# A four-layer gated attention kernel: one weight load in four transfers, a result stored in eight pieces, and a new instruction order on four engines

## The chip, the cores and the metric

The kernel runs on one core of a Trainium2 chip, in one launch. The metric is the device time of that launch in microseconds (us); where several runs are given, their median counts.

## What is computed

The input x holds 8 batches of 128 tokens with 128 features (float32). Four layers follow one another. Each adds a gated cross-attention and then a gated feed-forward network to x. In the code the eight steps are called A0, F0, A1, ROUTE with MOE, A2, F2, A3, F3:

```python
x = x + tanh(g_xattn[0]) * attention_16_heads_of_64(layernorm(x), ctx)   # A0, causal
x = x + tanh(g_ffn[0])   * ternary_gated_ffn(layernorm(x))               # F0
x = x + tanh(g_xattn[1]) * attention_16_heads_of_8(layernorm(x), ctx)    # A1, masked
x = x + tanh(g_ffn[1])   * top2_of_8_experts(layernorm(x))               # ROUTE, MOE
x = x + tanh(g_xattn[2]) * attention_1_head(layernorm(x), ctx)           # A2
x = x + tanh(g_ffn[2])   * ternary_ffn(layernorm(x))                     # F2
x = x + tanh(g_xattn[3]) * attention_16_heads_of_8(layernorm(x), ctx)    # A3
x = x + tanh(g_ffn[3])   * ternary_relu2_ffn(layernorm(x))               # F3
```

The ternary weights of F0, F2 and F3 are made from the loaded ones: their mean absolute value is needed first, then each weight is scaled, rounded and clipped. In the expert step every token goes to two of eight experts, and an expert takes at most 269 token rows, so that the step needs the routing of all eight batches before the first expert can run.

## The kernel before

Every batch is one tile of 128 tokens. All weights, the context and x lie in five packs in SBUF, loaded at the start over SyncE's one queue in the order: the first pack without x, x, the mask of A0, pack 1 (A0's weights wk, wq, wv, wo, 2048 KB, one transfer, semaphore `loaded[1]`), pack 2, pack 3 (the feed-forward weights, 2112 KB), the mask of A1, the lengths, pack 4. TensorE (PE) computes the keys of A1 first (`prepare`, L1006), then waits for the whole of pack 1, then begins A0.

Each engine runs one list of instructions in program order. The order is written out as numbers: every function of a step has a "place" for each of the eight batches, and `walk` emits the calls of one engine in rising order of place. The engines are tied by semaphores alone. A place is only a sort key: it is no time at which anything is started. VectorE's (DVE) functions of several instructions give up their turn after each instruction and come back 0.203 later in the list, so that two chains may interleave. The five engines' queues are SyncE (SP), GpSimd (POOL), ScalarE (ACT), PE and DVE.

```python
    while queue:
        at, n, begin, args = head = min(queue, key=lambda entry: entry[0:2])
        queue.remove(head)
        rest = begin(*args)
        if rest is not None:
            if next(rest, stages) is not stages:
                queue.append((at + TURN, n, lambda rest=rest: rest, ()))
```

Eight PSUM banks of 512 columns are shared: 0 and 1 for scores, 2 and 3 for transposed probabilities, 4 and 5 for attention outputs, 6 and 7 for the small projections. Before PE writes a bank, `claim` makes it wait until the piece that lay there before, by PE's own order, has been read out.

The names that matter in what follows, with b0 to b7 for the batches:

- `proj0` (L870, L865): the k, q and v projections of A0, each in two halves of 512 columns (k 0, k 1, q 0, ...). ACT copies k and q out (`k_sb`, `q_sb0`, L494), DVE copies v out (`v_sb`, L1239). The halves of k and v and the transposed x (`xt`, L763, copied out by ACT's `xt_sb`) share one bank.
- `scores0` (L772, L784): two groups of four heads at a time. DVE takes each row's maximum (`top_of`, L1228), ACT the exponentials and their sums (`exps`, L509), DVE the reciprocal (`recip0`, L1250), POOL the division (`norm0`, L433). PE then transposes (`probsT`, L828) and multiplies with v (`pv0`).
- `weights` on DVE (L1472): the absolute sums of the seven feed-forward weights. The first four wait for pack 3.
- `masks` on POOL (L390 to L402): masks of A1 and A2, built once, ahead of the first `norm0` in POOL's list.
- In MOE: PE's `xt_e`, `hidden` and `down` (L999) for each expert, ACT's gelu, DVE's `y_sb` (L1436), and POOL's `send` (L457), three indirect transfers per expert that put the rows back. When all 24 have landed, SP loads the rows batch by batch (L370), DVE adds them to x (`sum_stats`), POOL normalises (`rs`, L418 and L427), and A2 begins with `xt`.
- `fold` on DVE (L1505 to L1510): scales F2's second weight.
- `resid_q` of F3 (L1218): the last write of x. SP then stores x in one transfer of 512 KB (L374).

## Time and profile before

| | |
|---|---|
| three runs | 441.52, 441.66 and 443.7 us, median 441.66 us |
| the profiled execution | 440.93 us |
| its span, first to last instruction | 439.1 us |
| around the span | 1.83 us |
| PE busy | 376.0 us, 86% of the span |
| DVE, ACT, POOL busy | 287.6, 259.2 and 173.2 us |
| mean granted TensorE clock | 0.945 of full speed |

The busy times are of one execution. The span runs from the first to the last instruction that the profiler saw; the device time adds what lies around it. Shares over the whole span mix steps with different limits, so the trace is read stretch by stretch.

### The profile page before, as it was taken

Reading aid. Unit: us, or ns where it says so; the run is one execution under the profiler, and the core shown is the slowest. Engines: PE = TensorE matmul, PEld = TensorE weight load, DVE = VectorE, ACT = ScalarE, POOL = GpSimd, SP = SyncE. Lnnn points to the kernel's source line nnn. Section 1 sums busy time; section 2 is a strip of 40 time slices with the busy share of each in tenths; the row PEclk is TensorE's granted clock in tenths of the full one; section 3 lists DMA queues with packets and bytes.
Section 4 is the critical chain, followed back from the end, with each engine's and each line's share of the span. In section 5 each row is a group of like instructions: output and inputs, shape, how many; then the busy total and the mean of one; then the engine's idle time right before and its main releaser. Section 6 shows DMA issues by size and latency. Waiting matters only on the chain. (4 is left out here: it accounts for less than half of the span.)

```text
span 439.1 us, 9961 instructions
## 1 busy us (share of the span) xinstructions
PE 376.0 (86%) x3550; PEld 276.3 (63%) x3564; DVE 287.6 (65%) x872; ACT 259.2 (59%) x779; POOL 173.2 (39%) x232
## 2 busy tenths in 40 slices
PE   3689999999999999999985699961879999999843
PEld 1557877877778665655653289950656777776622
DVE  2254648998878888665565712214776487999994
ACT  3147667676686878867762644221575767556642
POOL 4494423524335410242467106664766333321120
PEclk9999999999999999999997679995799999999965
DMA  8990000000040000000000405113000000000001
GB/s 336 390 319 2 2 1 0 2 2 2 2 144 3 1 2 1 1 8 8 14 26 30 122 9 167 34 31 104 1 1 0 4 1 2 1 1 4 2 1 48
DMA packets 8711, 20.13 MB, mean 46 GB/s; under 512 B 1359, under 2 KB 5999, under 8 KB 8151
## 3 DMA queue, kind: packets, MB, share of 16 engines
q1 hardware_dynamic: 7383, 17.33, 11.2%
q0 software_dynamic: 1280, 2.17, 1.6%
q8 instruction: 29, 0.48, 0.5%
q14 instruction: 19, 0.16, 0.1%
HBM read 14.63 MB, written 4.87 MB: 44 GB/s over the span
## 5 line engine op out<-in xcount | busy, mean ns | idle before, releaser
L509 ACT ACTIVATE prob<-bank,mx 128x128 f32<-128x128 f32 x256 | 81.6, 379 | 23.3 <-DVE mx L1228 21.4
L1228 DVE TENSOR_REDUCE mx<-bank 128x4 f32<-128x512 f32 x96 | 63.6, 679 | 26.2 <-PE bank L801 19.3
L418 POOL TENSOR_TENSOR rstd<-mv,minus_half 128x1 f32<-128x1 f32 x64 | 36.9, 580 | 88.8 <-DVE mv L1203 88.5
L433 POOL TENSOR_TENSOR prob<-prob,rden 128x512 f32<-128x512 f32 x32 | 33.6, 1054 | 62.5 <-DVE rden L1250 62.5
L494 ACT ACTIVATE probT<-bank 128x512 f32<-128x512 f32 x64 | 39.0, 620 | 9.2 <-PE bank L828 9.0
L828 PE MATMUL bank<-pack,prob 128*128 128x128 f32 x256 | 39.5, 278 | 2.9 <-ACT prob L509 1.4
L828 PEld LDWEIGHTS bank<-pack,prob 128*128 128x128 f32 x256 | 28.5, 141 | 11.5 <-issue 6.1
L457 POOL DMA_INDIRECT yrows_d<-o_n,y_to x24 | 22.2, 925 | 31.0 <-DVE y_to L1424 18.8
L427 POOL TENSOR_SCALAR xn<-pack,mv,rstd 128x128 f32<-128x128 f32 x32 | 25.9, 809 | 10.3 <-PE bank L763 5.1
L509 ACT ACTIVATION_READ_ACCUMULATOR prob<-bank,mx 128x1 f32 x128 | 27.4, 214 | 0.0
L801 PE MATMUL bank<-kz,qz 64*128 64x512 f32 x96 | 26.8, 634 | 0.3 <-issue 0.2
L850 PE MATMUL bank<-probT,vz 128*32 128x128 f32 x512 | 26.8, 281 | 0.1
L853 PE MATMUL bank<-probT,pack 128*32 128x128 f32 x512 | 25.7, 273 | 0.0
L1239 DVE COPY va<-bank 128x512 f32<-128x512 f32 x16 | 11.0, 686 | 21.0 <-PE bank L865 20.9
L870 PE MATMUL bank<-pack 128*128 128x128 f32 x128 | 19.8, 303 | 4.4 <-DMA pack<-pack_d 2.7
L527 ACT ACTIVATE probT<-bank 128x512 f32<-128x512 f32 x32 | 18.2, 597 | 8.3 <-PE bank L816 7.7
L870 PEld LDWEIGHTS bank<-pack 128*128 128x128 f32 x128 | 17.2, 208 | 7.5 <-DMA pack<-pack_d 4.3
L870 PEld LDWEIGHTS bank<-xnT,pack 128*128 128x128 f32 x128 | 17.1, 201 | 6.0 <-issue 3.3
L494 ACT ACTIVATE xnT<-bank 128x128 f32<-128x128 f32 x40 | 11.3, 284 | 15.9 <-PE bank L763 15.7
L772 PE MATMUL bank<-neg,identb 128*128 128x512 bf16 x64 | 20.0, 381 | 0.7 <-ACT prob L509 0.4
L1210 DVE SCALAR_TENSOR_TENSOR pack<-bank,tanh_g,pack 128x128 f32<-128x128 f32 x40 | 13.8, 344 | 8.2 <-PE bank L913 5.4
L784 PEld LDWEIGHTS bank<-k,qT 64*128 64x128 f32 x256 | 15.5, 187 | 5.7 <-issue 5.2
(236 smaller groups left out, 936.2 us busy)
## 6 DMA issues: line engine op xcount, KB each, us to landing
pack<-pack_d SPq DMA_DIRECT2D x1, 2112.0 KB, 15.9
expert<-experts_d SPq DMA_DIRECT2D x4, 514.0 KB, 4.2
pack<-experts_d SPq DMA_DIRECT2D x4, 514.0 KB, 4.3
pack<-pack_d SPq DMA_DIRECT2D x1, 2048.0 KB, 10.4
xrows_d<-moe_rows SPq DMA_DIRECT2D x1, 1096.9 KB, 10.8
moe_rows<-xrows_d SPq DMA_DIRECT2D x8, 137.1 KB, 3.0
pack<-pack_d SPq DMA_DIRECT2D x1, 1044.0 KB, 5.2
pack<-pack_d SPq DMA_DIRECT2D x1, 1024.0 KB, 19.4
```

The source lines that it names most:

```text
L418: pool.tensor_tensor(rstd[layer][:, k, 0:1], mv[layer][:, k, 1:2], minus_half, ALU.pow).then_inc(ev.sem, 1)
L427: pool.tensor_scalar(out, x_sb[:, it.b, :], mv[layer][:, k, 0:1], rstd[layer][:, k, 0:1], ALU.subtract, ALU.mult).then_inc(ev.sem, 1)
L433: pool.tensor_tensor(part, part, r.to_broadcast([P, GH, P]), ALU.mult).then_inc(E[A0]["norm"].sem, 1)
L457: pool.indirect_dma_start(yrows_d, bass.IndirectOffsetOnAxis(ap=y_to[0:SP_, it.b, c:c + 1], axis=0), y_out[0:SP_, it.k, P * c:P * c + P], ...
L494: act.activation(dst, src, ACT.Identity if kw else ACT.Copy, **kw).then_inc(E[layer][name].sem, 1)
L509: act.activation(prob[:, g % 2, P * j:P * j + P], bank[S_BANK[g % 2]][:, P * j:P * j + P], ACT.Exp, bias=mx[:, g % 2, j:j + 1], **kw).then ...
L801: pe.matmul(bank[S_BANK[a]][:, :].rearrange("p (h t) -> p h t", h=GH), qz[rows, it.k, c, :], kt[c if layer == A3 else 0][rows, it.b, :, :] ...
L828: mm_ = pe.transpose(bank[T_BANK[g % 2]][:, P * j:P * j + P], prob[:, g % 2, P * j:P * j + P], ident)
L850: pe.matmul(out[QW * j:QW * j + QW, 0:P], vz[:, it.k, QW * h:QW * h + QW], probT[:, g, P * j:P * j + P], start=(g == 0), stop=(g == G - 1) ...
L853: mm_ = pe.matmul(out[QW * j:QW * j + QW, P:2 * P], col["sumsel"][:, QW * ROWS_OF[g]:QW * ROWS_OF[g] + QW], probT[:, g, P * j:P * j + P], ...
L870: mm_ = pe.matmul(out[:, P * t:P * t + P].rearrange("p (a n) -> p a n", a=1), w[:, 512 * c + P * t:512 * c + P * t + P], rhs, start=True, ...
L1228: dve.tensor_reduce(out, bank[S_BANK[g % 2]][:, :].rearrange("p (h t) -> p h t", h=GH), AX.X, ALU.max, negate=True).then_inc(E[layer]["max ...
```

## The change

Pack 1 is loaded in four transfers of 512 KB, each with a semaphore of its own, and PE waits for each part where batch 0 first needs it. PE's wait for the whole pack is gone. The result is stored in eight transfers of 64 KB, each after the last write of its batch. All places are new on POOL, ACT, PE and DVE: the same instructions, in another order. Counted over the lists, 79 of POOL's 145 calls, 209 of ACT's 378, 378 of PE's 579 and 330 of DVE's 453 stand at another position than before, most by one to four positions. Nothing is computed differently.

```diff
+        att_loaded = [sem(f"att_loaded{n}") for n in range(len(PACK_ATT0))]
...
-            sp.dma_start(packed[1][:, :], packs[1]).then_inc(loaded[1], 16)
+            for n in range(4):
+                part = slice(H * DK0 * n, H * DK0 * (n + 1))
+                sp.dma_start(packed[1][:, part], packs[1][:, part]).then_inc(att_loaded[n], 16)
...
-            wait(sp, F3, "resid", Item(B - 1, B - 1))
-            sp.dma_start(out_d, col["x"]).then_inc(stored, 16)
-            sp.wait_ge(stored, 16)
+            for b in range(B):
+                wait(sp, F3, "resid", Item(b, b))
+                sp.dma_start(out_d[:, P * b:P * b + P], x_sb[:, b, :]).then_inc(stored, 16)
+            sp.wait_ge(stored, 16 * B)
...
# PE, proj0
+                if it.rep == 0:
+                    pe.wait_ge(att_loaded["kqv".index(which)], 16)
# PE, y0
+                if it.rep == 0:
+                    pe.wait_ge(att_loaded[3], 16)
# PE, prepare
-                pe.wait_ge(loaded[1], 16)
```

Of the places, the entries that the prediction speaks of (one number for each batch):

```diff
# ACT
-                    (k_sb, 0, (-64.674, 6.532, 33.177, 68.417, 81.955, 97.344, 109.162, 130.381)),
-                    (q_sb0, 1, (0.966, 47.21, 60.706, 78.743, 93.317, 107.974, 118.994, 143.209)),
+                    (k_sb, 0, (-37.074, 2.832, 36.777, 60.917, 78.355, 98.644, 110.762, 130.581)),
+                    (q_sb0, 1, (4.166, 46.51, 53.206, 77.943, 97.017, 110.574, 117.594, 138.709)),
...
-                    (xt_sb, A2, (305.399, 309.837, 317.659, 324.065, 325.465, 338.97, 344.481, 352.645)),
-                    (exps2, (305.658, 318.513, 320.097, 327.004, 339.204, 342.353, 352.51, 356.392)),
+                    (xt_sb, A2, (295.399, 296.037, 312.059, 312.765, 322.965, 336.27, 341.681, 346.745)),
+                    (exps2, (299.958, 303.513, 318.097, 325.904, 334.104, 337.753, 352.31, 354.692)),
# PE
-                    (proj0, 'k', 0, (-68.338, 16.554, 33.651, 62.844, 75.296, 86.591, 103.178, 124.066)),
-                    (scores0, 0, (5.828, 44.126, 61.419, 76.871, 92.365, 106.553, 123.441, 136.216)),
+                    (proj0, 'k', 0, (-71.338, 2.954, 28.351, 59.444, 73.696, 86.791, 104.378, 123.966)),
+                    (scores0, 0, (5.128, 37.026, 59.919, 78.871, 91.565, 106.153, 121.841, 135.116)),
# DVE
-                    (top_of, A0, 1, (28.558, 45.502, 66.943, 78.474, 99.664, 121.184, 132.098, 143.564)),
-                    (recip0, 0, (33.527, 46.729, 70.002, 79.044, 102.997, 121.118, 133.935, 143.635)),
+                    (top_of, A0, 1, (14.658, 38.202, 63.143, 81.374, 100.964, 118.984, 131.898, 145.964)),
+                    (recip0, 0, (8.027, 39.429, 64.402, 83.544, 103.997, 120.018, 134.135, 145.935)),
...
-            walk(stages, [(65.7, means), (267.418, weigh_experts), (268.718, keys3_sb), (312.818, fold), (273.8, squared_bias)])
+            walk(stages, [(59.1, means), (264.618, weigh_experts), (264.918, keys3_sb), (289.618, fold), (233.8, squared_bias)])
# POOL
-                    (send, 0, (274.765, 279.806, 285.746, 292.887, 295.527, 295.868, 299.308, 303.049)),
-                    (send, 1, (278.812, 283.352, 286.593, 294.633, 295.774, 295.914, 299.755, 308.295)),
-                    (send, 2, (280.359, 284.899, 288.94, 295.18, 295.821, 298.461, 302.302, 310.042))],
+                    (send, 0, (263.965, 273.006, 281.746, 283.587, 292.527, 296.768, 301.208, 304.749)),
+                    (send, 1, (277.312, 280.752, 282.293, 286.433, 294.274, 297.114, 302.955, 305.295)),
+                    (send, 2, (280.159, 280.899, 285.34, 290.08, 294.921, 299.961, 312.102, 312.542))],
```

Sorted, this means among other things:

- PE begins `proj0` k 0 of b1 ahead of the first `scores0` of b0, and not behind it. ACT copies that k 0 out ahead of `q_sb0` 1 of b0.
- DVE runs the first `recip0` of b0 ahead of its second `top_of`. The four weight sums still stand between `v_sb` 0 and `v_sb` 1 of b0.
- POOL runs the first `norm0` of b0 ahead of the `rs` of b2; `masks` still stands ahead of both.
- At the end of MOE, PE runs `down` of expert 6 behind all `hidden` of expert 7, directly ahead of the last `down`. POOL's last sends are, by expert and part, 6.0, 6.1, 7.0, 7.1, 6.2, 7.2, where they were 6.0, 6.1, 6.2, 7.0, 7.1, 7.2.
- DVE runs `fold` in the middle of MOE, where it stood behind the `sum_stats` of b2. ACT runs `xt_sb` of b1 in A2 ahead of `exps2` of b0, where it stood behind it. PE transposes b2 ahead of the first `probsT2`.

## Rows read from the trace of the kernel before

**Rows 1.** Page, parts 1 and 5: busy us, share; groups with busy, mean ns, idle before.

```profile
PE 376.0 (86%) x3550; PEld 276.3 (63%) x3564; DVE 287.6 (65%) x872; ACT 259.2 (59%) x779; POOL 173.2 (39%) x232
...
L509 ACT ACTIVATE prob<-bank,mx 128x128 f32<-128x128 f32 x256 | 81.6, 379 | 23.3 <-DVE mx L1228 21.4
L1228 DVE TENSOR_REDUCE mx<-bank 128x4 f32<-128x512 f32 x96 | 63.6, 679 | 26.2 <-PE bank L801 19.3
...
L433 POOL TENSOR_TENSOR prob<-prob,rden 128x512 f32<-128x512 f32 x32 | 33.6, 1054 | 62.5 <-DVE rden L1250 62.5
```

**Rows 2.** Windows by stretch: length, busy us (instructions) per engine, granted clock, DMA share, GB/s.

```profile
20.00:60.00 40.00, 37.56 (x302) 28.10 (x303) 20.31 (x50) 24.97 (x102) 22.54 (x25) 1.00 0.31 103
...
285.00:300.00 15.00, 7.60 (x58) 6.64 (x56) 1.24 (x4) 2.68 (x6) 8.32 (x9) 0.95 0.10 29
300.00:320.00 20.00, 12.30 (x63) 9.36 (x63) 15.00 (x62) 9.11 (x31) 12.53 (x18) 0.70 0.17 53
...
400.00:420.00 20.00, 17.15 (x275) 12.98 (x269) 19.37 (x65) 11.03 (x23) 3.78 (x8) 1.00 0.01 2
```

**Rows 3.** Timeline 0 to 32 us: start, length, engine, line, operation, count, idle before.

```profile
1.62 0.42 SPq L336 DMA_DIRECT2D mask_u<-mask_d  x1
...
3.31 0.49 SPq L340 DMA_DIRECT2D pack<-pack_d  x1
...
6.00 3.78 PE L1006 MATMUL bank<-pack 128*128 128x512 f32 x4 [6.00 <-DMA pack<-pack_d]
...
12.53 2.07 PE L870 MATMUL bank<-pack 128*128 128x128 f32 x8 [2.75 <-DMA pack<-pack_d]
...
23.04 2.46 DVE L1472 TENSOR_REDUCE asum<-pack 128x1 f32<-128x512 f32 x4
...
24.67 1.16 PE L784 MATMUL bank<-k,qT 64*128 64x128 f32 x16
24.99 6.21 POOL L402 TENSOR_SCALAR neg<-pack,lens_f,qneg 128x128 bf16<-128x128 f32 x8
...
26.15 1.16 PE L870 MATMUL bank<-pack 128*128 128x128 f32 x8 [0.32 <-DVE va L1239]
```

**Rows 4.** DMA issues: tiles, queue, count, KB each, median us from issue to landing.

```profile
pack<-pack_d SPq DMA_DIRECT2D x1, 2112.0 KB, 15.9
...
pack<-pack_d SPq DMA_DIRECT2D x1, 2048.0 KB, 10.4
...
moe_rows<-yrows_d SPq DMA_DIRECT2D x8, 128.0 KB, 2.4
...
out_d<-pack SPq DMA_DIRECT2D x1, 512.0 KB, 2.6
...
mask_u<-mask_d SPq DMA_DIRECT2D x1, 128.0 KB, 6.0
```

**Rows 5.** Timeline 30 to 48 us.

```profile
35.13 0.66 PE L828 MATMUL bank<-pack,prob 128*128 128x128 f32 x4
...
46.66 1.16 PE L784 MATMUL bank<-k,qT 64*128 64x128 f32 x16
```

**Rows 6.** Timeline 287 to 326 us, around the expert stage's end.

```profile
290.44 2.83 PE L999 MATMUL bank<-pack,k 128*90 128x128 f32 x24 [0.67 <-ACT k L613]
...
297.00 0.93 POOL L457 DMA_INDIRECT yrows_d<-o_n,y_to  x1 [0.31 <-issue]
...
303.99 0.82 DVE L1505 TENSOR_SCALAR projw<-t_projT,pack 128x128 f32<-128x128 f32 x4
...
304.22 0.47 PE L763 MATMUL bank<-pack 128*128 128x128 f32 x1 [10.95 <-POOL pack L427]
...
306.30 1.28 ACT L558 ACT_TABLE_LOAD   x1 [1.29 <-DVE mx L1262]
...
307.95 0.27 ACT L494 ACTIVATE pack<-bank 128x128 f32<-128x128 f32 x1
```

**Rows 7.** Timeline 427 us to the end.

```profile
436.10 0.34 SPq L374 DMA_DIRECT2D out_d<-pack  x1
```

More of the change, by code:

```diff
@@ new lines, in _ @@
+                    (v_sb, A3, (369.17, 375.27, 387.425, 398.861, 417.874, 428.162, 439.436, 459.711)),
+                    (exps3, 0, (374.856, 385.637, 393.573, 409.51, 422.989, 430.576, 443.752, 464.38)),
+                    (exps3, 1, (374.858, 385.739, 399.274, 409.664, 424.553, 431.589, 450.665, 466.674)),
+                    (exps3, 2, (378.377, 388.974, 402.71, 410.823, 425.611, 435.785, 453.06, 469.239)),
+                    (exps3, 3, (381.171, 389.869, 404.604, 412.016, 427.104, 439.178, 455.753, 470.533))],
@@ new lines, in _ @@
+                    (probsT, A0, 1, (29.713, 58.078, 70.271, 86.65, 101.487, 117.775, 133.362, 149.067)),
+                    (probsT, A0, 2, (33.997, 61.191, 77.743, 88.437, 108.282, 121.97, 137.057, 150.054)),
+                    (probsT, A0, 3, (37.196, 61.941, 82.74, 92.535, 108.623, 125.31, 138.285, 152.38)),
+                    (pv0, 0, (39.433, 63.178, 82.278, 89.872, 108.56, 122.047, 138.837, 150.932)),
+                    (pv0, 1, (44.778, 65.87, 84.833, 95.26, 114.647, 133.435, 143.841, 154.153)),
@@ new lines, in _ @@
+                ROUTE: [
+                    (xt, ROUTE, (185.917, 207.711, 212.815, 225.419, 234.523, 243.948, 256.272, 259.34)),
+                    (logits, (195.66, 210.763, 221.067, 229.271, 238.464, 246.536, 256.325, 259.4)),
+                    (places, (201.127, 211.93, 222.934, 234.138, 241.963, 254.872, 257.835, 261.242)),
+                    (keys3, (None, None, None, None, None, None, None, 261.692)),
+                    (fold, (None, None, None, None, None, None, None, 263.502))],
@@ new lines, in _ @@
+                    (scores, A3, 0, (359.468, 370.054, 382.383, 395.772, 403.2, 416.774, 427.442, 443.333)),
+                    (top_T, 0, (362.333, 372.454, 386.084, 398.473, 408.047, 420.579, 429.87, 444.961)),
+                    (scores, A3, 1, (366.414, 373.14, 390.069, 398.758, 408.633, 422.964, 431.755, 448.046)),
+                    (scoresT, 0, (366.665, 373.292, 390.087, 399.776, 412.45, 423.382, 432.273, 448.464)),
+                    (top_T, 1, (368.617, 377.043, 392.332, 402.159, 411.534, 424.301, 438.092, 450.063)),
@@ new lines, in _ @@
+                    (recip0, 3, (36.061, 62.166, 79.132, 96.35, 116.847, 127.467, 140.362, 162.404)),
+                    (ot_sb0, 0, (37.878, 64.928, 87.884, 100.865, 122.79, 140.104, 153.041, 164.795)),
+                    (ot_sb0, 1, (40.529, 71.466, 91.715, 110.432, 124.855, 142.468, 160.928, 169.204)),
+                    (resid, A0, (60.78, 80.028, 94.801, 116.537, 133.058, 145.97, 162.128, 173.78))],
+                F0: [
+                    (ln_stats, F0, (64.651, 89.736, 98.754, 116.775, 136.287, 146.817, 162.297, 173.891)),
+                    (quant0, (66.478, 95.997, 118.521, 125.835, 138.692, 162.005, 167.651, 176.491)),
+                    (gate0, (92.128, 114.731, 128.152, 142.864, 161.995, 172.676, 178.369, 195.338)),
+                    (hid0, (96.211, 119.21, 132.23, 145.653, 162.419, 174.961, 182.516, 195.541)),
+                    (resid_q, F0, (112.093, 128.415, 143.727, 160.968, 173.736, 180.118, 193.535, 208.901))],
```

345 lines of the change are left out of this document (158 added, 187 removed).

## Prediction

> **What bounds the kernel now.** I read the page's busy times first: PE works 376.0 of 439.1 us, and nothing else comes near it [rows 1]. So the question is where PE's 63.1 idle us lie, and which of them the change can reach. The windows by stretch answer it. From 20 to 60 us PE is busy 37.56 of 40 us and there an edit that spares another engine's wait buys nothing by itself. Around the end of the expert stage PE is busy 7.60 of 15 and then 12.30 of 20 us, the latter at a granted clock of 0.70. From 400 to 420 us DVE is the full engine, 19.37 of 20 us [rows 2]. Third, the timeline of the start: PE has nothing until 6.00, computes A1's keys until 9.78, and then stands 2.75 us for pack 1, until 12.53 [rows 3]. Fourth, the timelines at the end of the expert stage and of the kernel: PE waits 10.95 us there for the first normalised tile of A2 [rows 6], and the one store is issued at 436.10 [rows 7] and lands 2.6 us later [rows 4].
>
> So the change can reach a wait of 2.75 us at the start, some of the idle time around A2's start, and the store. All the rest is order.
>
> **Part 1: four transfers.** Mask 0, ahead of pack 1 in the queue, is issued at 1.62 [rows 3] and lands 6.0 us later [rows 4], at 7.62. Pack 1's 2048 KB land at 12.5, so they take 4.9 us, 1.22 us for each 512 KB. The parts land at about 8.85 (wk), 10.1 (wq), 11.3 (wv) and 12.5 (wo). PE is with A1's keys until 9.78, so k 0 of batch 0 starts at about 9.85 and not at 12.53: 2.7 us. The three additional issues cost SP about 0.42 us each [rows 3], 1.3 us, and push the issues of packs 2, 3 and 4 back by as much; pack 3, issued at 3.31 [rows 3], lands 15.9 us later [rows 4], so its data stands some 9 us in the queue behind the rest, and that covers the 1.3 us. Without that cover pack 3 would land 1.3 us later.
>
> Next comes what the 2.7 us run into. DVE's list still has the first four weight sums between `v_sb` 0 and `v_sb` 1 of b0. They wait for pack 3 at 3.31 + 15.9 = 19.2. Before, they ran from 23.04 for 2.46 us, and k 0 of b1, whose bank waits for `v_sb` 1 behind them, started at 26.15, that is 0.65 us after them [rows 3]. Now everything in front of them is ready by then; they run from 19.2 to 21.7, and k 0 of b1 starts at 22.3: a lead of 3.8 us. But the scores of b0, which ran from 24.67 [rows 3], now stand behind this k 0 on PE. With about 0.95 us for k 0 and 0.5 us for the mask they start at 23.8: lead 0.9 us. Behind them the softmax is a chain of latencies: maximum 0.68, four exponentials of 0.38 (1.5 in all), reciprocal, division 1.05 [rows 1]. `recip0` now holds the second maximum on DVE until the first exponentials are done, and POOL cannot divide before its masks end at 24.99 + 6.21 = 31.2 [rows 3]. First division 31.2 to 32.25. PE's first `probsT` is not bound by it: the second scores and v 1 of b1 stand ahead of it, and by the same durations they end at about 33.3. It ran at 35.13 [rows 5], so the lead is 1.8 us. Then k 1 of b2 waits on ACT behind the exponentials of the third group, some 1.3 us. The second scores of b1, at 46.66 before [rows 5], come at about 46.0. The lead is 0.7 us there, from where on PE is nearly full again and keeps it. My steps are rough by half a microsecond each. The bounds are nothing (the division and the sums take it all) and 2.75 us (the wait is gone, and nothing takes its place). I take 1.2, nearer to the worked-out 0.7.
>
> The Trainium skill, "DMA: Bandwidth & Descriptors", section "Anatomy of one DMA", gives each transfer a fixed cost of some 2 us, and its section "Bandwidth" advises to batch to 1 MiB or more. That speaks against four pieces of 512 KB: by its figure three more transfers add some 6 us if they pay in turn, and nothing if they overlap. In this trace packs 1, 2 and 3 follow one another at the pace of the bytes; the third rival works that out from rows.
>
> **Part 2: the order from 47 to 241 us.** Here the same instructions run on a PE that is busy about 94% of the time at its start [rows 2] and more behind that. I found no call moved ahead of what it needs by more than a few positions. The idle time is some 2.5 us in 40, so the order can win or lose about 2 us in all. I take zero, from -2 to +2.
>
> **Part 3: the end of MOE.** PE's last `down` waited 0.67 us for a gelu [rows 6]; the other `down` now stands ahead of it and covers that: -0.67. POOL sends part 2 of expert 6 behind two sends of expert 7. These can't start before the last `down` is copied out, so four sends follow it and not three. One takes 0.93 us plus 0.31 us of issue [rows 6]: +1.24. Sum +0.6, between 0 (the send slips into a gap of POOL) and +1.2. SP waits for all 24 sends, and the whole of A2 waits for SP.
>
> **Part 4: the start of A2.** `fold` (0.82 us for its four scalings, and two more short ones, about 1.4 in all) ran on DVE at 303.99, in the middle of the first batches' statistics. In MOE DVE is nearly idle (1.24 of 15 us from 285 us on [rows 2]) and hides it; with that cover gone it costs the 1.4 us again. ACT copied b1's transposed tile at 307.95 only, as its table load at 306.30 and `exps2` of b0 stood ahead [rows 6]. Now the copy goes first, at about 306.3, and `exps2` comes 0.3 us later. So b1 gains 1.65 us and b2 about 1.2 us of statistics, and b0 loses 0.3. In 300 to 320 us PE is idle 7.7 us, of which 4.2 lie before 304.22 [rows 2, 6]; 3.5 us is the most that can be filled. I take -1.8, half of that, between 0 and -3.5.
>
> **Part 5: F2 to F3.** PE, then DVE, are full, and the sum of their work is the same: 0, from -1.5 to +1.5.
>
> **Part 6: the store.** Seven stores of 64 KB go out while later batches compute. The last one is issued as before and carries an eighth of the bytes. The nearest rows: 512 KB stored in 2.6 us, 128 KB loaded in 2.4 us [rows 4]. At pack 1's pace 448 KB fewer are 1.1 us. So the gain is 0.2 to 1.1; I take 0.6. Eight waits on SP hold nothing up, as SP has nothing else left.
>
> **Sum.** -1.2 + 0 + 0.6 - 1.8 + 0 - 0.6 = -3.0 us, on the profiled execution's 440.93 (span 439.1 and 1.83 around it) 437.9. The median of the three runs, 441.66, lies 0.73 above that execution, so I predict 438.7 us, 0.67% less. I count a difference under 0.5% (439.45 to 443.87) as none: about what a measurement of this kernel can tell from no change.
>
> **The rivals.**
>
> The lead is kept (chance 0.17). The whole 2.75 us survive to 47 us, because a division or an exponential comes sooner than my chain has it, A2's front gains 2.5 us, and the order wins 1 us in A0 to A1: -2.75 - 1 + 0.6 - 2.5 - 0.6 = -6.2, 435.4 us. For it: the wait of 2.75 is the longest of PE behind the first load that isn't forced by data. Against it: POOL's masks end at 31.2 whatever PE does [rows 3].
>
> Nothing is left (0.24). The lead is gone by 47 us, A2's front gives 0.6, the send costs 0.6, and only the store's 0.6 stays, with up to 1 us either way from the order: 440.1 to 442, centre 441.1 us. For it: PE is nearly full between 47 and 220 us, so it has no slack to give; DVE's end doesn't move if its work comes no sooner.
>
> The transfers pay in turn, and it is slower (0.10 with every other loss). A load of 128 KB alone takes 2.4 us [rows 4] and would need 0.3 us at pack 1's pace; so some 2 us are fixed. Were they paid by each part in turn, pack 3 would land 6 us later, at 25.2, the sums end at 27.7, and k 0 of b1 start at 28.3. The scores behind it start at 29.8 and not 24.67: +5.1, less about 1.5 us that the masks until 31.2 hide. +3.6 - 0.6 + 0.6 - 0.5 = +3.1: 444.8 us. It decides once pack 3 lands more than about 1 us after 19.2, because k 0 now stands ahead of the scores. Against it: packs 2 and 3, 670 and 2112 KB, land within 19.2 - 12.5 = 6.7 us, as fast (415 KB/us) as pack 1 alone (418 KB/us) [rows 3, 4].
>
> My own sum has 0.49, with its own range 437.0 to 440.3.
>
> **How the numbers follow.** The low end takes most of the first rival, 435.0; the high end all of the second and stops short of the third, 442.6. Faster by over 0.5%: 0.17 and most of the 0.49 (0.42) make 0.59. No difference: the rest of the 0.49 and 0.24 make 0.31. Slower: 0.10.
>
> **What would show it.** k 0 of batch 0 at about 9.9 us, with no wait on a load of pack 1 behind it; the weight sums at 19.2 to 19.5; k 0 of b1 at 22.3, ahead of the scores at 23.8; the first `probsT` at about 33.3, the second scores of b1 at 46.0. In MOE four sends behind the last `down`; in A2 no `fold` between the statistics and a copy of b1's tile ahead of the table load. From A2's first `xt` to the last `resid_q`, before 304.22 to about 436, 1.5 to 2 us less. The last store 1.5 to 2.4 us from issue to landing. I would be wrong if PE idles more than 3 us more than before between 47 and 241 us, if pack 3 lands after 20.5, or if DVE's new list leaves it waiting in F3, where it was full.

## The result, and the profile after

The changed kernel takes 445.48 us (median of six runs, 444.51 to 446.54) against 441.61 us of six runs of the kernel before: ratio 1.0081, 95% interval 1.0055 to 1.0106. Timed once more beside other kernels it gave 1.0085 (1.0053 to 1.0117). By the ratio it is slower by 3.6 us; the medians lie 3.9 us apart. I had predicted 438.7 us. The profiled execution has a span of 443.3 us against 439.1.

The windows over the stretches of [rows 2], of the kernel after (same columns), with one more for the first 20 us:

```profile
0.00:20.00 20.00, 10.17 (x37) 6.62 (x38) 5.92 (x19) 5.92 (x10) 7.87 (x17) 0.90 0.92 360
20.00:60.00 40.00, 35.17 (x278) 26.43 (x279) 18.82 (x48) 21.73 (x88) 22.15 (x25) 0.92 0.31 108
...
285.00:300.00 15.00, 11.44 (x90) 10.58 (x88) 2.34 (x9) 3.81 (x9) 9.24 (x10) 0.97 0.11 32
300.00:320.00 20.00, 9.54 (x35) 6.60 (x35) 10.49 (x40) 5.27 (x18) 9.94 (x14) 0.51 0.22 60
...
400.00:420.00 20.00, 18.03 (x275) 13.38 (x280) 18.96 (x63) 11.68 (x26) 2.61 (x6) 1.00 0.04 12
```

From 20 to 60 us PE is busy 35.17 us and not 37.56, with 278 instructions and not 302, at a granted clock of 0.92 and not 1.00. That is where to look first. The timeline of the start, of the kernel after, answers to [rows 3, 5]:

```profile
5.02 0.45 SPq L343 DMA_DIRECT2D pack<-pack_d  x1
...
9.41 1.16 PE L876 MATMUL bank<-pack 128*128 128x128 f32 x8
...
18.74 2.07 PE L876 MATMUL bank<-xnT,pack 128*128 128x128 f32 x8 [0.69 <-ACT qT L498]
19.93 2.47 DVE L1479 TENSOR_REDUCE asum<-pack 128x1 f32<-128x512 f32 x4 [2.86 <-DMA pack<-pack_d]
...
20.60 1.91 PE L871 MATMUL bank<-pack 128*128 128x512 f32 x2
...
22.55 0.69 DVE L1246 COPY va<-bank 128x512 f32<-128x512 f32 x1 [0.16 <-PE bank L871]
23.30 1.16 PE L876 MATMUL bank<-pack 128*128 128x128 f32 x8 [0.78 <-DVE va L1246]
24.50 0.60 ACT L498 ACTIVATE k<-bank 128x512 f32<-128x512 f32 x1 [5.81 <-PE bank L876]
24.82 1.16 PE L788 MATMUL bank<-k,qT 64*128 64x128 f32 x16
24.99 0.59 ACT L498 ACTIVATE qT<-bank 128x512 f32<-128x512 f32 x1
...
28.12 0.60 ACT L498 ACTIVATE k<-bank 128x512 f32<-128x512 f32 x1
28.87 0.30 PE L767 MATMUL bank<-pack,xn 128*128 128x128 f32 x1 [1.80 <-ACT k L498]
29.54 2.07 PE L876 MATMUL bank<-xnT,pack 128*128 128x128 f32 x8 [0.37 <-ACT xnT L498]
...
35.63 0.60 PE L832 MATMUL bank<-pack,prob 128*128 128x128 f32 x4
...
39.20 1.16 PE L876 MATMUL bank<-pack 128*128 128x128 f32 x8 [1.03 <-ACT k L498]
...
48.43 1.16 PE L788 MATMUL bank<-k,qT 64*128 64x128 f32 x16
```

The row of the kernel before that answers to the one at 28.87, the transposed x of b1:

```profile
29.97 0.30 PE L763 MATMUL bank<-pack,xn 128*128 128x128 f32 x1 [0.82 <-ACT k L494]
```

k 0 of b0 starts at 9.41 us, 3.1 us sooner than before. At 18.74 PE runs q 1 of b0, which ends at 20.8, and at 20.60 v 1, both at TensorE's lower clock level, 1.2 GHz. PE starts k 0 of b1 at 23.30 only, when DVE has copied the second half of v behind its weight sums; in this execution that copy waits for v 1 itself as well (22.55). The scores of b0 stand behind k 0 of b1 and begin at 24.82; they began at 24.67 before [rows 3]. ACT's copy of q 1 stands behind that of k 0 of b1, and ACT idles 5.81 us ahead of the two. But the first scores wait for the first copies of q and k alone, and they begin ahead of the copy of q 1 (24.99). So the order on PE holds them, and not that copy.

Then ACT's copy of k 1 of b1 (28.12) stands behind four exponentials, and PE idles 1.80 us for it, where it idled 0.82 before. The eight products at 29.54 take 2.07 us where eight like them took 1.16 at 23.30: the clock is at 1.2 GHz from 29.6 to 33.0 us. The transposed x of b1 still has a lead of 1.1 us (28.87; 29.97 before). Behind the slow stretch the first `probsT` has none (35.63; 35.13 before). After it PE waits 1.03 us for ACT's copy of k 0 of b2 (39.20) and 0.35 for a copy of v, where the kernel before has no such wait, and the second scores of b1 run at 48.43 (46.66 before [rows 5]).

The DMA issues of the kernel after (columns as in [rows 4]):

```profile
pack<-pack_d SPq DMA_DIRECT2D x5, 512.0 KB, 7.6
pack<-pack_d SPq DMA_DIRECT2D x1, 2112.0 KB, 14.9
...
out_d<-pack SPq DMA_DIRECT2D x8, 64.0 KB, 1.6
```

Pack 3, issued at 5.02, lands at 19.9, 0.7 us later than before. The stores land in 1.6 us (median of eight) and not in 2.6.

The end of the expert stage, timeline of the kernel after, answers to [rows 6]:

```profile
291.04 2.78 PE L1007 MATMUL bank<-expert,k 128*90 128x128 f32 x24
...
293.66 2.78 PE L1007 MATMUL bank<-pack,k 128*90 128x128 f32 x24
...
295.09 0.92 POOL L461 DMA_INDIRECT yrows_d<-o_n,y_to  x1 [1.66 <-DVE y_to L1431]
296.32 0.93 POOL L461 DMA_INDIRECT yrows_d<-o_n,y_to  x1 [0.30 <-issue]
...
297.71 0.92 POOL L461 DMA_INDIRECT yrows_d<-o_n,y_to  x1 [0.47 <-issue]
298.94 0.93 POOL L461 DMA_INDIRECT yrows_d<-o_n,y_to  x1 [0.31 <-issue]
300.17 0.92 POOL L461 DMA_INDIRECT yrows_d<-o_n,y_to  x1 [0.30 <-issue]
301.40 0.93 POOL L461 DMA_INDIRECT yrows_d<-o_n,y_to  x1 [0.30 <-issue]
...
308.74 0.48 PE L767 MATMUL bank<-pack 128*128 128x128 f32 x1 [12.30 <-POOL pack L431]
```

The last `down` starts 3.2 us later than before (290.44), the last send 4.4 us later (297.00), A2's first tile 4.5 us later (304.22). Four sends follow the last `down`, as I had said.

To see where time is lost, the starts of a few fixed calls are compared. The table gives, for each kernel's profiled execution, the start of a call minus its start before (us), and the ratio of the times with its interval, each against runs of before on the same chip. The first `probsT` is that of b0; y0 is the last product of A0 for a batch; "places b7" ends ROUTE.

| kernel | first probsT | y0 b2 | y0 b5 | y0 b7 | places b7 | last down | A2 first xt | last resid_q | span | ratio (95%) |
|---|---|---|---|---|---|---|---|---|---|---|
| before (start) | 35.13 | 83.13 | 136.16 | 155.51 | 241.59 | 290.44 | 304.22 | 435.72 | 439.1 | |
| after | +0.51 | +2.52 | +2.65 | +4.15 | +3.85 | +3.21 | +4.52 | +5.22 | 443.3 | 1.0081 (1.0055 to 1.0106) |
| e1 four transfers, old order | -0.30 | -0.41 | -0.54 | -0.54 | -0.48 | -1.11 | -1.15 | -1.39 | 437.7 | 0.9978 (0.9955 to 1.0001) |
| e2 stores, old order | -0.13 | -0.14 | -0.13 | -0.13 | -0.47 | -0.37 | -0.34 | -0.30 | 437.8 | 0.9992 (0.9970 to 1.0013) |
| e3 new order, one transfer | +2.98 | +5.04 | +5.17 | +6.66 | +6.36 | +5.73 | +6.83 | +7.52 | 445.6 | 1.0161 (1.0126 to 1.0196) |
| e4 old order to 45 us | -0.74 | -0.05 | +0.09 | +1.59 | +1.55 | +0.53 | +1.84 | +2.51 | 440.6 | 1.0018 (0.9997 to 1.0040) |
| e8 old order to 245 us | +0.76 | +0.72 | +0.59 | +0.59 | +0.64 | -1.16 | +0.09 | +1.51 | 439.6 | 0.9970 (0.9952 to 0.9989) |
| e6 scores first | -1.46 | +0.57 | +0.72 | +2.22 | +1.97 | +1.28 | +2.66 | +3.40 | 441.5 | 1.0009 (0.9988 to 1.0029) |
| e5 old order, masks later | -1.18 | -1.24 | -1.22 | -1.23 | -0.87 | -0.76 | -0.71 | -0.67 | 437.5 | 0.9917 (0.9886 to 0.9949) |
| e17 as e5, A2's front | -2.98 | -3.02 | -3.13 | -3.13 | -2.51 | -2.90 | -2.95 | -2.97 | 435.2 | 0.9941 (0.9913 to 0.9969) |

Read along the row "after": 0.5 us are lost until the first `probsT`, 2.0 more until y0 of b2, 1.3 more until the end of ROUTE, 0.6 come back in MOE, 1.3 go between the last `down` and A2, 0.3 come back until F3's last transposed tile (430.84 us, 426.60 before), 1.0 go at the very end (to the last `resid_q`), and the shorter store gives back 1.0. The sum is the span's 4.2 us.

Three of these losses are the same in every trace with the new order at that place, and absent from every trace with the old one (all runs below counted, e7's seam apart). From the first `probsT` to y0 of b0 the new order takes 16.8 us (16.2 in e13) and the old one 15.5 to 15.6. From y0 of b0 to y0 of b1 it is 17.0 against 16.2. From y0 of b5 to y0 of b7 it is 20.85 against 19.35, 1.5 us (1.9 in e13, which edits that stretch). The first `probsT` itself differs between executions of one order: e10, e14 and e16 have the changed kernel's lists there, and it came at +1.67, +1.59 and +1.31, where the row "after" has +0.51. Their stretches at 1.2 GHz lie elsewhere (15.9 to 22.8 and 29.6 to 33.0 us in the changed kernel's trace, 23.8 to 27.2 and 30.6 to 34.0 in e16's).

### The profile page after: what moved, and what is told of

It reads as the page before. It is cut to its first block, busy times and chain, and to the rows that moved or that the text cites. A ratio compares the mean times of both kernels' runs of the same rounds, so it can differ in the third digit from the quotient of the medians.

```text
span 443.3 us, 9977 instructions
## 1 busy us (share of the span) xinstructions
PE 378.6 (85%) x3547; PEld 276.6 (62%) x3564; DVE 284.3 (64%) x872; ACT 259.4 (59%) x779; POOL 172.9 (39%) x232
## 4 chain that ended last, share of the span: by engine, by line
PE 65%; DVE 14%; ACT 10%; issue 6%; DMA 2%; POOL 2%; another core or an unknown queue 0%; DVEq 0%; ACTq 0%; SPq 0%; POOLq 0%
PE bank L805 8%; ACT prob L513 5%; PE bank L832 5%; PE bank L876 5%; PE bank L1007 4%; PE bank L998 4%; PE bank L820 3%; PE bank L871 3%; PE bank L788 3%; PE bank L854 3%; PE bank L776 3%; PE bank L857 2%; DVE mx L1235 2%; PE bank L887 2%; PE bank L767 2%
## 5 line engine op out<-in xcount | busy, mean ns | idle before, releaser
L513 ACT ACTIVATE prob<-bank,mx 128x128 f32<-128x128 f32 x256 | 81.2, 378 | 29.6 <-DVE mx L1235 27.1
L461 POOL DMA_INDIRECT yrows_d<-o_n,y_to x24 | 22.2, 927 | 31.5 <-DVE o_n L1443 20.1
L453 POOL DMA_INDIRECT xrows_d<-xn_all,row_of x16 | 16.4, 1025 | 27.0 <-DVE row_of L1409 24.1
L498 ACT ACTIVATE xnT<-bank 128x128 f32<-128x128 f32 x40 | 11.2, 280 | 22.7 <-PE bank L767 22.6
L876 PEld LDWEIGHTS bank<-xnT,pack 128*128 128x128 f32 x128 | 18.6, 216 | 6.6 <-issue 4.3
L776 PE MATMUL bank<-neg,identb 128*128 128x512 bf16 x64 | 21.0, 381 | 1.6 <-ACT prob L513 1.4
L498 ACT ACTIVATE pack<-bank 128x128 f32<-128x128 f32 x24 | 6.3, 279 | 25.4 <-PE bank L767 21.8
L876 PE MATMUL bank<-xnT,pack 128*128 128x128 f32 x128 | 19.9, 306 | 1.1 <-ACT qT L498 0.7
L876 PE MATMUL bank<-pack 128*128 128x128 f32 x128 | 18.0, 283 | 3.2 <-ACT k L498 1.7
L871 PE MATMUL bank<-pack 128*128 128x512 f32 x32 | 19.2, 685 | 1.4 <-ACT xnT L498 1.4
```

The costliest lines, as they stand in the source:

```text
L498: act.activation(dst, src, ACT.Identity if kw else ACT.Copy, **kw).then_inc(E[layer][name].sem, 1)
L513: act.activation(prob[:, g % 2, P * j:P * j + P], bank[S_BANK[g % 2]][:, P * j:P * j + P], ACT.Exp, bias=mx[:, g % 2, j:j + 1], **kw).then ...
L776: pe.matmul(bank[S_BANK[g % 2]][:, :].rearrange("p (h t) -> p h t", h=GH), identb[:, :], (neg0 if layer == A0 else neg1)[:, bass.ds(it.b, ...
L871: mm_ = pe.matmul(out[:, :], ctxT[:, it.b, :], col["wvT_0"][:, 512 * c:512 * c + 512], start=True, stop=True)
L876: mm_ = pe.matmul(out[:, P * t:P * t + P].rearrange("p (a n) -> p a n", a=1), w[:, 512 * c + P * t:512 * c + P * t + P], rhs, start=True, ...
```

## The experiments

My theory after the result (A): the new order at the start spends the lead and more. The rivals: the four transfers cost the time themselves (B), or the later order does (C). The first four kernels take the change apart.

**e1, four transfers alone.** The places, and with them the order, of before.

```diff
 # before, with only this of the change
-            sp.dma_start(packed[1][:, :], packs[1]).then_inc(loaded[1], 16)
+            for n in range(4):
+                part = slice(H * DK0 * n, H * DK0 * (n + 1))
+                sp.dma_start(packed[1][:, part], packs[1][:, part]).then_inc(att_loaded[n], 16)
```

> The order of before, with the four transfers alone (one store, as before). Theory A (the new order of the start spends the lead): with the old order the first k starts at about 9.4 us instead of 12.53, nothing is held back behind it, and the kernel takes 438.5 to 441.5 us. Rival B (starting PE early on part of the weights costs the time by itself, as PE runs dry and its granted clock falls to 0.5 once more): a second stretch at 0.5 behind 22 us here too, and 443 to 446 us.

**e2, the stores alone.** Before, with the eight stores.

```diff
-            sp.dma_start(out_d, col["x"]).then_inc(stored, 16)
...
+            for b in range(B):
+                wait(sp, F3, "resid", Item(b, b))
+                sp.dma_start(out_d[:, P * b:P * b + P], x_sb[:, b, :]).then_inc(stored, 16)
```

> Before, with the store batch by batch alone. The last store then lands about 1 us sooner after its issue (2.6 us before, 1.6 us in the changed kernel): 440.4 to 441.0 us. Rival: the end of the kernel waits for something else, and it stays at 441.6.

**e3, the new order with one transfer.** The changed kernel without its four transfers.

```diff
-            for n in range(4):
-                part = slice(H * DK0 * n, H * DK0 * (n + 1))
-                sp.dma_start(packed[1][:, part], packs[1][:, part]).then_inc(att_loaded[n], 16)
+            sp.dma_start(packed[1][:, :], packs[1]).then_inc(loaded[1], 16)
```

> The changed kernel with pack 1 in one transfer again, order and stores as changed. Theory A: the order alone loses the time, and k 0 of batch 1 stands behind the weight sums (19.9 us) in either case: 444.5 to 447 us. Rival B (the four transfers lose it): 440.5 to 442.5 us.

**e4, the old order at the start.** The changed kernel; the calls that before begins within 45 us have before's order on all four engines: their places are those of before, all others the new ones plus 2000. One line of ACT and one of PE:

```diff
-                    (q_sb0, 1, (4.166, 46.51, 53.206, 77.943, 97.017, 110.574, 117.594, 138.709)),
+                    (q_sb0, 1, (0.966, 47.21, 2053.206, 2077.943, 2097.017, 2110.574, 2117.594, 2138.709)),
...
-                    (scores0, 0, (5.128, 37.026, 59.919, 78.871, 91.565, 106.153, 121.841, 135.116)),
+                    (scores0, 0, (5.828, 44.126, 2059.919, 2078.871, 2091.565, 2106.153, 2121.841, 2135.116)),
```

> The changed kernel in which the calls that the kernel before begins within 45 us stand in the order of before on all four engines; all behind them in the new order. Theory A: the swing of 5 us between 27 and 42 us is gone, and 440 to 442 us are left of 445.5. Rival B: 444.5 to 446. Rival C (the loss is spread over the later order, between 110 and 180 us, and the start only takes the lead): 442.5 to 444.

B falls: with the old order the four transfers give 0.9978 (up to 1.0001), about 1 us, and with the new one 3.3 us (1.0161 against 1.0081). The new order with one transfer costs 1.6%, more than A had. e4 gives back 2.8 us of the 3.6 by the ratios, the larger part, as A has it. Its 442.61 us lie above A's range and at the low end of C's, though: the later order costs time too, and e8 says how much. The store's own gain (0.9992) is under what the runs can tell, though its trace ends 1.0 us sooner after the last `resid_q`.

Why do the four transfers give 1 us and not the 2.8 us by which PE starts earlier? The timeline of e1, PE and POOL:

```profile
21.20 1.16 PE L787 MATMUL bank<-k,qT 64*128 64x128 f32 x16
...
26.02 6.23 POOL L405 TENSOR_SCALAR neg<-pack,lens_f,qneg 128x128 bf16<-128x128 f32 x8
...
33.73 2.04 POOL L436 TENSOR_TENSOR prob<-prob,rden 128x512 f32<-128x512 f32 x2
...
34.83 0.66 PE L831 MATMUL bank<-pack,prob 128*128 128x128 f32 x4 [2.42 <-POOL prob L436]
```

The scores of b0 keep the lead (21.20 against 24.67), but the first division stands behind POOL's masks and one `rs` behind them, and PE waits 2.42 us for it. **e5** has the old order, the four transfers and the eight stores, and moves the eight masks of A2, which nobody reads before A2, behind; **e15** does so with pack 1 in one transfer.

```diff
-                for b in range(B):
-                    pool.tensor_scalar(neg2[:, b, :], ...)       # eight in a row in masks()
+            def mask2(b):
+                pool.wait_ge(pool_const, 7)
+                pool.tensor_scalar(neg2[:, b, :], ...)
...
-            walk(stages, [(-52.8, masks)])
+            walk(stages, [(-52.8, masks)] + [(175.0 + 5 * b, lambda b=b: mask2(b)) for b in range(B)])
```

> The order of before, four transfers, store batch by batch, and POOL's eight masks of A2 (6.2 us in a row, until 32.2 us) moved from ahead of the first division to single places from 175 us on. Theory A (what is left of the early start, some 2.4 us, is held up by POOL's masks alone: PE's wait for the first division in e1_four_only): PE's first probsT at about 32.4 us instead of 34.83, and 438 to 439.2 us. Rival B (the lead is lost at the next wait anyway, ACT's or DVE's): 440 to 441 us, like the four transfers with the old masks.

> Before, with stores by batch and the masks of A2 later, but with pack 1 in one transfer. Theory A (the masks only hold the lead of the four transfers back; without it PE's first transposes waited for nothing at 35.13 us): 440.5 to 441.6 us, ratio 0.997 to 1.000. Rival F (the masks also delay batch 0 and 1 in the kernel before, and moving them is the whole gain of e5): 438.5 to 439.5 us, ratio 0.992 to 0.995.

e5 took 438.76 us beside 442.33, ratio 0.9917: faster than both kernels. PE's wait for the first division is gone; the first `probsT` came at 33.95 in its execution and at 32.14 in that of e17, whose start is the same. e15 came out at 0.9953 (0.9928 to 0.9979), between the two expectations. Its trace shows nothing gained until the end of ROUTE (first `probsT` -0.25, y0 of b7 -0.21, places b7 +0.55), so rival F's mechanism is not there, but what made its runs quicker than those of e2 I did not find. What the masks are worth beside the four transfers can be read where two executions spent the same time at 1.2 GHz at the start. With 3.4 us of it y0 of b2 starts at 82.73 in e1, and at 80.45 and 80.12 in e12 and e17, which have e5's start. With 10.2 us it starts at 83.85 in e8, which has e1's start, and at 81.90 in e5. That is 2.0 to 2.6 us, as much as the wait of 2.42.

**e6, two calls put back.** The changed kernel; on PE the first scores of b0 ahead of k 0 of b1, on ACT the copy of q 1 of b0 ahead of that of k 0 of b1.

```diff
-                    (q_sb0, 1, (4.166, 46.51, 53.206, 77.943, ...
+                    (q_sb0, 1, (2.5, 46.51, 53.206, 77.943, ...
...
-                    (scores0, 0, (5.128, 37.026, 59.919, 78.871, ...
+                    (scores0, 0, (2.5, 37.026, 59.919, 78.871, ...
```

> The changed kernel with two calls put back at the start: on PE the first scores of batch 0 ahead of k 0 of batch 1, on ACT the copy of q 1 of batch 0 ahead of that of k 0 of batch 1. Theory A1 (these two hold the scores of batch 0 until pack 3 has landed and the weight sums are done): scores at about 22 us instead of 24.82, the copy of k 1 of batch 1 is no longer held behind four exponentials, no stretch at clock 0.5 behind 29 us, and 1.5 to 2.5 us less: 443 to 444 us. Rival A2 (the loss comes after the first probsT, from the second maximum behind v 1 of batch 1, and POOL's masks hide the earlier scores): 445 to 445.8 us.

The ratio is 1.0009: these two numbers out of some 1,550 hold 3.2 of the 3.6 us by the ratios, more than I expected. By the two traces it is 2.0 us at y0 of b2 and 1.8 at the span's end. With more executions it is 2.0 to 4.5: y0 of b2 starts at 85.65, 86.46, 86.75 and 86.81 in the changed kernel, e16, e14 and e10, and at 83.70 and 82.33 in e6 and e13, which has e6's start. The means are 3.4 us apart. PE's timeline in e6:

```profile
20.45 1.16 PE L788 MATMUL bank<-k,qT 64*128 64x128 f32 x16
...
23.09 1.16 PE L876 MATMUL bank<-pack 128*128 128x128 f32 x8 [1.48 <-DVE va L1246]
...
26.91 0.30 PE L767 MATMUL bank<-pack,xn 128*128 128x128 f32 x1 [0.82 <-ACT k L498]
27.58 2.08 PE L876 MATMUL bank<-xnT,pack 128*128 128x128 f32 x8 [0.37 <-ACT xnT L498]
```

The scores run 4.4 us sooner, k 0 of b1 hardly earlier, and the wait of 1.80 us for ACT's copy is 0.82 again. In e6's execution q 1 and v 1 of b0 ran at 2.4 GHz, in that of the changed kernel at 1.2. The changed kernel's second trace, e16, has them at 2.4 GHz as well:

```profile
17.79 1.16 PE L876 MATMUL bank<-xnT,pack 128*128 128x128 f32 x8 [0.69 <-ACT qT L498]
...
22.77 1.16 PE L876 MATMUL bank<-pack 128*128 128x128 f32 x8 [2.95 <-DVE va L1246]
...
24.70 2.08 PE L788 MATMUL bank<-k,qT 64*128 64x128 f32 x16
```

So the order moves the scores by 4.25 us, at most 0.4 of it the clock, which fell at 23.8 in e16: PE idles 2.95 us for the copy of v 1 behind the weight sums, with the scores ready behind k 0. The edit on ACT was not run by itself; as the first scores do not wait for the copy of q 1, it is the exchange on PE that brings them forward. One thing I had wrong: the stretch at 1.2 GHz is still there (27.58, 2.08 us).

**e9, the sums behind the copy of v** (the diff; `v_sb` 1 of b0 stands at -14.87), and **e11,** the edit of e6 and that of e5 together.

```diff
-                    (weights, (-22.753, -29.144, 49, 76.941, ...
+                    (weights, (-14.4, -14.5, 49, 76.941, ...
```

> The changed kernel in which only DVE's eight weight sums of batches 1 and 0 (which wait for pack 3 until 19.9 us and last until 22.4) stand behind the second copy of v of batch 0, not ahead of it. Theory A1a (k 0 of batch 1 waits for that copy, the scores and ACT stand behind it): k 0 of batch 1 at 22.2 us instead of 23.30, the scores at 23.7 instead of 24.82; but the maxima then stand behind the sums, so that at most 1 us comes back: 444.3 to 445.2 us at the 441.6 of before, ratio 1.006 to 1.008. Rival A1b (the time of the k alone decides, and its order before the scores does no harm): 442.5 to 443.5 us, ratio 1.002 to 1.005, as with scores first.

> The changed kernel with the scores first (as in e6) and POOL's eight masks of A2 in single places from 175 us on (as in e5). If the masks hold PE in the new order too: first probsT about 2 us earlier than in e6, and 439.5 to 441 us (at 441.6 of before), ratio 0.995 to 0.999. If in the new order it is ACT and DVE that hold it: 442 us, ratio 1.001.

e9: 1.0047 (1.0023 to 1.0070), but its trace doesn't show the mechanism: k 0 of b1 starts at 23.42, as late as before the edit, since v 1 itself, run at the lower clock, ends at 22.6. So this execution bears out neither theory, and what the order of the sums costs stays open: in e16 and e14, where v 1 ended at 19.8 and 20.0, k 0 of b1 waited 2.95 and 3.02 us for the copy behind them. e11: 1.0008 (0.9985 to 1.0031), the ratio of e6: in the new order the masks hold less than the times can tell. By the traces of e11 and e13, which spent as long at 1.2 GHz at the start, it is 0.4 us at y0 of b2 (81.92 and 82.33).

**e7 and e8, where the rest is lost.** The edit of e4, with the old order until 135 and until 245 us.

> The changed kernel with the calls that the kernel before begins within 135 us in the order of before, all later ones in the new order. By the lag of PE's work in the trace of e4_old_start the new order between 45 and 135 us loses 1.3 us: 441.0 to 441.8 us, between e4_old_start (442.6) and old_to_245. If what is lost there is given back later (PE waits at the end of ROUTE anyway): 442.3 to 443 us.

> The changed kernel with the old order until the expert stage, the new one only from MOE on (four transfers, stores by batch). If MOE to F3 in the new order cost nothing, as I had predicted with -1.2 us: 439 to 440.3 us (four transfers and stores alone give 440.3 to 441). If the later sends at the end of MOE cost 1.2 us and F3's order some more: 441.3 to 442.3 us.

e7 gave 1.0058 (1.0037 to 1.0079), worse than e4, which no theory had: its trace loses 4.9 us between y0 of b5 (-1.14) and y0 of b7 (+3.76), right behind the seam of the two orders. It tells of the seam and not of the change, and I drop it. e8 gave 0.9970, what four transfers and stores give together: by the ratios the new order costs nothing from MOE on, and the order between 45 and 245 us costs the difference to e4, 0.48% or 2.1 us. The traces agree: from the first `probsT` to the end of ROUTE e4 loses 2.3 us (-0.74 to +1.55) and e8 nothing (+0.76 to +0.64). Most of it is the 0.8 us between y0 of b0 and of b1 and the 1.5 between y0 of b5 and of b7.

**e13, two waits of the middle.** e6 with two more calls of PE put back.

```diff
-                    (up, F0, 'up', ..., (88.521, 106.625, 125.212, ...
+                    (up, F0, 'up', ..., (88.521, 106.625, 121.9, ...
...
-                    (probsT, A1, 0, (152.469, 167.509, ...
+                    (probsT, A1, 0, (153.2, 167.509, ...
```

> The scores-first kernel (e6) with two more calls of PE put back: the up product of F0's batch 2 ahead of the first pv of batch 5 (at about 120 us), and the first transposes of A1's batch 0 behind F0's ht of batch 4 (at 152.5 us). Theory D1 (the middle's loss is made of such single waits: 0.87 to 1.09 us for a bank that DVE's product with the up result frees, 1.11 us for ACT's exponentials): both waits gone from the trace and 1 to 2 us less than e6: ratio 0.9965 to 0.999. Theory D2 (PE is held by the other engines' order as a whole, and a wait taken away comes back some us later): the ratio of e6, 1.001.

1.0017 (0.9989 to 1.0044): no gain. In the trace the first exchange takes its wait of 0.87 us away; in place of the second wait (1.10) stands one of 1.57 for ACT's transposed copy, at the call now in front. So D2 is the nearer, and the middle's loss isn't settled call by call.

**e10 and e14, the end of MOE.** e10 is the changed kernel with the old order of the sends; e14 also puts `down` of expert 6 ahead of the last two hidden products of expert 7 (the second pair of lines).

```diff
-                    (send, 2, (280.159, ..., 299.961, 312.102, 312.542))],
+                    (send, 2, (280.159, ..., 299.961, 304.5, 312.542))],
...
-                    (down, (273.752, ..., 298.012, 306.652, 308.072))],
+                    (down, (273.752, ..., 298.012, 302.0, 308.072))],
```

> The changed kernel with POOL's third send of expert 6 put back ahead of the two first sends of expert 7. If the four sends behind the last down set A2's start: the last send 1.2 us earlier against the last down, A2's first transposed tile as much, and 444.0 to 444.8 us (at 441.6 of before), ratio 1.005 to 1.007. If the loads of the returned rows or the clock set it: the 445.2 of the changed kernel, ratio 1.008.

> The changed kernel with the old order of the sends (as e10) and, on PE, down of expert 6 ahead of the last two hidden products of expert 7. Theory E1 (POOL's last six sends run without a gap, 1.23 us each, from the copy of down 6 on, so that down 6 sets the last send): down 6 about 1.7 us earlier, the last send 6.5 us behind the last down and not 7.6, A2's first transposed tile 1.2 us earlier against the last down. Rival E2 (the last three sends behind the last down set it): 7.6 us as before, no change. In time: ratio 1.003 to 1.006 against 1.008 of the changed kernel.

In e10's trace the last send starts 7.58 us behind the last `down` (7.74 in the changed kernel, 6.56 before): POOL's last six sends run without a gap from 294.91 on, 1.23 us each, so their order doesn't matter. In e14:

```profile
291.15 2.78 PE L1007 MATMUL bank<-expert,k 128*90 128x128 f32 x24
...
295.52 2.83 PE L1007 MATMUL bank<-pack,k 128*90 128x128 f32 x24 [0.67 <-ACT k L617]
...
299.61 0.92 POOL L461 DMA_INDIRECT yrows_d<-o_n,y_to  x1 [1.02 <-DVE o_n L1443]
300.84 0.92 POOL L461 DMA_INDIRECT yrows_d<-o_n,y_to  x1 [0.30 <-issue]
302.07 0.93 POOL L461 DMA_INDIRECT yrows_d<-o_n,y_to  x1 [0.31 <-issue]
```

It is 6.55 us there, and E1 has the mechanism: the distance is 6.55 or 6.56 in every trace with `down` of expert 6 ahead of the last hidden products of expert 7, and 7.58 to 7.75 in all others. But PE's last `down` waits for the gelu again (0.67). From ROUTE's end to A2's first tile e14 loses nothing against before (+5.16 to +5.18) and the changed kernel 0.7 (+3.85 to +4.52), so some half of the 1.2 us is a gain; e10 gains 1.2 over the same stretch (+5.33 to +4.11), though, so executions differ there by more than the edit. The ratios, 1.0047 (1.0022 to 1.0073) and 1.0043 (1.0017 to 1.0068), are lower than the changed kernel's by more than the traces explain, as e9's is. To see whether the changed kernel's own ratio was a chance, it was run again:

> The changed kernel as it is, timed beside the next one, to place the variants that came out at 1.0043 to 1.0047. If the first comparison was a fair draw: ratio 1.007 to 1.009. If it was at the upper end of its interval: 1.004 to 1.006, and the two calls at the start are then worth 1.6 us and not 3.2.

1.0085. So the first comparison stands. The 1.5 us by which e9, e10 and e14 beat it have no cause that I can show; their intervals overlap the changed kernel's, which was timed beside none of them, so the 1.5 us may be no difference at all.

**e12 and e17, A2's front.** e12 has three parts: old order, from 245 to 322 us the new one (places plus 2000) with the old sends, old order again (plus 4000), on top of e5. e17 makes two edits in e5:

```diff
-                    (xt_sb, A2, (305.399, 309.837, ...
+                    (xt_sb, A2, (305.399, 305.5, ...
-            walk(stages, [..., (312.818, fold), ...])
+            walk(stages, [..., (289.618, fold), ...])
```

> The old order until 245 us with four transfers, stores by batch and the masks of A2 later (as e5); from there to 322 us the new order of the expert stage's end and A2's front, with the old order of the sends; behind that the old order again. If A2's new front (copy of the second tile ahead of the table load, fold in MOE) gains the 1.1 us that the lag of PE's work shows there, and the old F3 keeps it: 1 to 2 us under e5, ratio 0.987 to 0.990. If A2's front only makes up for a later start: the ratio of e5, 0.992.

> The old order with four transfers, stores by batch and the masks of A2 later (e5), and in it two calls at A2's front alone: ACT copies A2's transposed tile of batch 1 ahead of the exponentials of batch 0, and DVE's fold stands in MOE. My step on A2's front said -1.8 us (0 to -3.5): ratio 0.987 to 0.990. By the lags of the mixed kernels 1 us: 0.989 to 0.990. Rival: the copy gains what the exponentials of batch 0 lose, and fold was in nobody's way: the 0.992 of e5.

e12: 0.9939 (0.9913 to 0.9964), e17: 0.9941; neither beats e5. In e17's trace A2's first tile starts 2.95 us sooner than before and A2's last sums end 3.0 us sooner: the two edits give 0.05 us. The rival holds. In every trace A2's first tile starts 7.1 to 7.4 us behind the last send.

## Why the prediction was wrong

- **Part 1 is the step that failed.** I gave the first `probsT` 33.3 us, a lead of 1.8, and it came at 35.63 (36.44 to 36.80 in e10, e14 and e16). I had the parts' landing right (k 0 at 9.41, 9.85 said), pack 3 nearly (19.9, 19.2 said), the place of k 0 of b1 between the weight sums and the scores, and the later wait for ACT behind exponentials (1.03 us, 1.3 said). I gave the scores 23.8 and they came at 24.82: 0.7 us are pack 3's, and the rest came with v 1, which ran at 1.2 GHz. Then 10.8 us and not 9.5 went by until the first `probsT`. In e10, at 2.4 GHz from 28.0 us on, it was 9.5 (27.29 to 36.80); here 29.6 to 33.0 us ran at 1.2 GHz, a term that my sum put at nothing. What I had priced wrong is the order: with the scores put first, the first `probsT` came at 33.67 and 32.95 (e6, e13), the lead that I had promised for the order that holds them back. My "-1.2 (0 to -2.75)" became +1.8 us at the second scores of b1. The bounds failed more than the value: I took "nothing left" for the worst case.
- **What stays open in part 1** is whether the waits bring the lower clock. In the changed kernel, e9, e14 and e16 the clock falls at 29.6 to 30.6 us, within 1 us after PE's wait of 1.6 to 1.8 us for the copy of k 1; in e10, with the same wait, it does not fall, and in e6 it falls with a wait of 0.82.
- **ACT's exchange** cost nothing that the trace shows. The Trainium skill, "PSUM — Partial Sum Buffer", section "Engine vs sequencer instructions", says that ScalarE's queue is strictly first in, first out. The row at 24.50 agrees: ACT idles 5.81 us, the last 3.7 of them with a finished q 1 behind.
- **The third rival had the mechanism and the wrong trigger.** I wrote that k 0 ahead of the scores costs time once pack 3 lands over 1 us late. It landed 0.7 us late, and the loss was there. None of the three signs that I had named for being wrong appeared: of the loss, 1.8 us lay in the part that I held for a sure gain, and 2.1 in part 2, under the 3 us that I had set as the sign.
- **The rival "the lead is kept"** was set aside for POOL's masks until 31.2 us. e1 shows it: with the old order they take 2.42 us of the lead.
- **Part 2** (0, from -2 to +2): from the second scores of b1 to the end of ROUTE +2.1 us in the trace (+1.77 to +3.85), and 2.1 by e4 and e8. That is just past the upper bound; the order was not as harmless as I took it for.
- **Part 3** (+0.6): -0.6 until the last `down` and +1.3 behind it, +0.7. The size was right, the reason half: `down` of expert 6, moved back by two products, delays all six sends, not the order of the sends (e10, e14).
- **Part 4** (-1.8): e17 gives 0.05. From A2's first tile to F3's last the changed kernel gains 0.3. What holds A2's front instead was not looked for.
- **Part 5** (0): F3's end loses 1.0 in the trace, within the bounds.
- **Part 6** (-0.6): -1.0 in the traces of the changed kernel and of e2, near the upper bound. Three more loads in the queue cost pack 3 0.7 us. The Trainium skill, "DMA: Bandwidth & Descriptors", section "Anatomy of one DMA", counts some 2 us fixed for each transfer, measured on GpSimd's path. The eight stores of 64 KB, issued by SP, landed in 1.6 us, so the measurement is lower here.

Worked out with what the trace showed: +1.77 + 2.08 + 0.67 + 0.70 (A2 to F3's end) - 1.03 = +4.19 us, the difference of the spans.

## What to carry to other kernels

A wait that is taken away at the start is worth what the next waits leave of it: follow the earlier data through every engine's list (here ACT's copies and POOL's masks), not only through the engine that waited. Where a list is reordered, look for a call that now stands in front of ready work and needs something late (here k 0 of b1 in front of the scores); a single such pair can cost more than the change gains, and the bounds must then reach to the slower side. Where executions differ by the clock, compare several of each list, over stretches at one clock level: there the losses of an order came out alike to a few hundredths of a us. A reorder of many calls is best taken apart by putting the old order back up to some point, but the seam can cost more than the order, so look at it in the trace.

## What the hardware showed that I had not expected

TensorE's granted clock differs between executions of the same order by as much as the edits here are worth. e5 and e17 have the same lists until MOE. Their windows from 28 to 34 us, e5 first:

```profile
28.00:34.00 6.00, 6.00 (x31) 3.85 (x31) 1.53 (x4) 1.90 (x9) 3.01 (x4) 0.72 0.65 229
```

```profile
28.00:34.00 6.00, 6.00 (x47) 4.37 (x46) 2.63 (x7) 2.63 (x13) 3.36 (x4) 1.00 0.68 237
```

PE is busy for the whole 6 us in both, with 31 instructions at a mean clock of 0.72 and with 47 at 1.00. The first has two stretches at 1.2 GHz in its first 32 us (14.5 to 21.3, 28.1 to 31.5), the second one (15.2 to 18.6), and 1.8 to 1.9 us of difference stay until the end of A0 (y0 of b7 -1.23 and -3.13). They ran on two chips; e12, on the chip of e5 and with the same start, has one stretch (16.3 to 19.8) and its y0 of b7 at -2.80. Twelve runs of one kernel lie up to 3.7 us apart (e1: 438.78 to 442.49); the fastest ran at a mean clock of 0.948 and the four slowest at 0.930. That is not all of it: two runs of the kernel before took 440.0 and 443.65 us, both at 0.941. So one trace is no measure of a 1 us edit at the start. The Trainium skill, "TensorE: Matmul & The Clock Gate", section "What's actually happening", says that the point of the rise varies from run to run of one kernel and puts the whole loss under 1% of a span. The traces agree with the first; for the second, the 1.8 us are 0.4% of the span, and that is the size of most effects here.
